# The last step of a gated feed-forward stage: its selection and last product reordered, its result added and stored tile by tile, and a weight split moved one step on

## The chip, the core and the metric

The kernel runs on one core of a Trainium2 chip. The metric is device time in microseconds (us) of one launch, as the median of the runs shown. Engines carry two names: TensorE is PE (its weight loads PEld), VectorE DVE, ScalarE ACT, GpSimd POOL, SyncE SP.

## What is computed

Two transformer-like layers on x of (4, 512, 512), each with an attention part and a feed-forward part behind a layer norm whose scale, shift and gate come from a conditioning vector. The change concerns the feed-forward part of the second layer, cut here to what matters:

```python
def _sparsify_2to4(h):                      # I = 2048
    g = h.reshape(B, S, I // 4, 4)
    a = jnp.abs(g)
    _, idx = jax.lax.top_k(a, 2)
    pos = jnp.arange(4)
    mask = (pos == idx[..., 0:1]) | (pos == idx[..., 1:2])
    return (g * mask.astype(g.dtype)).reshape(B, S, I)
h = silu(x @ w_gate) * (x @ w_up)           # w_gate, w_up: (512, 2048)
y = _sparsify_2to4(h) @ w_down              # w_down: (2048, 512)
...
x = x + gb * y                              # gb: one row of 512 for each batch
```

Of every four neighbouring hidden values the two of larger magnitude are kept, and the output is a float32 array (4, 512, 512).

## The kernel before

One program walks through stages A (attention), B (experts), C (the second layer's first part) and D, the feed-forward part above. `walk` gives each engine the same sequence of steps: in stage D four groups g of 512 hidden columns (the first and the last written out, the middle two a loop), and in each group the four batches b, 512 rows each. Each engine's instructions run in the order in which its own `step_d` emits them; engines meet at semaphores (`wait_ge`, `then_inc`). There is no planner: where an instruction stands in its function is where it stands in its queue.

Every float32 product is made of three matmuls on rounded parts (`mm3`, lines 768 to 772): HI times HI, HI times LO, LO times HI. So each operand is first split: ScalarE copies it rounded (HI), and GpSimd or VectorE subtracts that copy from the value (LO).

A step (g, b) of stage D:

- TensorE computes gate and up for four blocks r (the hidden columns are laid out so that the four members of each group of four sit in blocks 0 to 3), 24 matmuls a block, into banks 0 and 4 or 1 and 5. So block r=2 needs the banks of r=0 back. Then it runs the down product of the step before (`tail_d`, from line 1167): four tiles t of 128 rows, 12 matmuls each, 48 in all, into two banks that take turns (a ring).
- ScalarE applies SiLU to each gate block (L1580), takes absolute values (L1566, into `ab4`), and after the selection makes the HI copies into `ad` (L1605). For the last three groups, step b=0 ends with the HI copies of the down weights (`split_d(g, 4)` and `(g, 5)`, L1235, into W2). Their LO parts are on GpSimd's queue at the end of the same step (L2239). TensorE waits for them at the down product of b=0, which stands in step b=1.
- VectorE multiplies SiLU by up (L2172, into `hh`), then selects: comparisons, maxima and minima of the pairs (0, 1) and (2, 3), flags, and four products of flag and value (L2219). Between these it evacuates the four tiles of the previous down product, times the gate row, into `tmp` (L1898).
- GpSimd adds each `tmp` to x (L2305) and makes the LO parts of `ad` (L2239), but in the last step of all, where VectorE makes them (L2226).
- SyncE loads the raw weights (L560) and stores a finished batch as one transfer of 1024 KB (L754).

The last step (g=3, b=3) has nothing behind it but its own down product: `epi` on TensorE runs it, VectorE evacuates its four tiles, GpSimd adds them, and SyncE stores the batch.

Of the kernel before, what the change touches and what calls it, by code (L numbers as in the profile page):

```python
# [26 lines left out]
ALU = mybir.AluOpType  # L27
# [212 lines left out]
def build(nc, x_in, wa, wbe, wdn, winout, coef, cT, wmod0, wmod1, gwT, bo, norm_w, out, rows_d_):  # L240
# [4 lines left out]
    with ExitStack() as ctx:  # L245
# [124 lines left out]
        hb = [xnb[:, :].rearrange("p (t n) -> p t n", t=NT), h1[:, :, :], h2[:, 0, :, :], h2[:, 1, :, :]]  # L370

# [174 lines left out]
        def _(sp):  # L546
# [204 lines left out]

            def store(b):
# [4 lines left out]
            def epi():  # L757
                store(3)
                sp.wait_ge(out_stored, 16 * NB)
                for stored in row_stored:  # L760
                    sp.wait_ge(stored, 16)
# [5 lines left out]
        def _(pe):  # L767
# [399 lines left out]
            def tail_d(g, b, n0):  # L1167
                s = g * NB + b
                pe.wait_ge(d_lo, s * 4 + 4)
                if b == 0:  # L1170
                    pe.wait_ge(split_done, split_d_at(g, 5) + 1)
                for t in range(NT):
                    o = ring_slot(n0 + t, par_of("D", g, b, t))
                    for r in range(4):
                        last = mm3(o[:, :], lambda h, r=r: ad[:, r, h, t * P:(t + 1) * P],
# [35 lines left out]
        def _(act):  # L1211
# [341 lines left out]
            def step_d(g, b):  # L1553
# [14 lines left out]
                for r in range(4):  # L1568
# [11 lines left out]
                    act.activation(hh[:, r, :], bank[r % 2][:, :], ACT.Silu).then_inc(d_silu, 1)  # L1580
                    if b == 3 and not (isinstance(g, int) and g == GD - 1):
# [16 lines left out]
                if tail_of("D", g, b):  # L1598
                    act.wait_ge(ring_full, ring_before("D", g, b) + NT)
# [3 lines left out]
                for r in range(4):  # L1603
                    act.wait_ge(d_sp, s * NSP + (NSP - 3 + r))
                    act.activation(ad[:, r, HI, :], hh[:, r, :], ACT.Copy).then_inc(d_hi, 1)  # L1605
                if b == 0 and not first:
                    split_d(g, 4)
                    split_d(g, 5)
# [5 lines left out]
        def _(dve):  # L1614
# [548 lines left out]
            def step_d(g, b):  # L2163
# [5 lines left out]
                for r in range(4):  # L2169
                    dve.wait_ge(du_full, s * 4 + (r + 1))  # L2170
                    dve.wait_ge(d_silu, s * 4 + (r + 1))
                    dve.tensor_tensor(hh[:, r, :], hh[:, r, :], bank[4 + r % 2][:, :], ALU.mult).then_inc(d_h, 1)  # L2172
                    if opening and r == 0:
                        add_normed(3, 2)
                        add_normed(3, 3)
                        c_stats(3, 3)
                    if opening and r == 1:
                        c_scales((3, 3))
# [12 lines left out]
                dve.wait_ge(d_abs, s * 4 + 2)  # L2191
                op(tt(c01, a[0], a[1], ALU.is_ge))
                op(tt(mx[:, :], a[0], a[1], ALU.max))
                tail_evac("D", g, b, 0)
                op(tt(a[0], a[0], a[1], ALU.min))
# [4 lines left out]
                tail_evac("D", g, b, 1)  # L2200
                op(tt(a[2], a[2], a[3], ALU.min))
# [393 lines left out]
```

## Time and profile before

| | |
|---|---|
| median of 3 runs | 1926.1 us (1924.27 to 1926.55) |
| profiled execution, as timed | 1928.25 us |
| its span, first to last instruction | 1925.8 us |
| mean granted TensorE clock | 0.970 |
| TensorE busy | 1798.4 us, 93% of the span |
| VectorE busy | 1179.9 us, 61% |
| ScalarE, GpSimd busy | 754.3 and 688.0 us, 39% and 36% |

The rows of a timeline give start, length, engine, line, operation and tiles (output <- inputs, buffer numbers left out), and in brackets how long the engine had been idle and what ended it. Consecutive instructions of an engine may overlap in the record; the distance of two starts is then what an instruction costs. Ends of matmuls are modelled. The granted clock is 1.0 at 2.4 GHz and 0.5 at 1.2 GHz.

### The profile page before, as it was taken

The page shows a single profiled execution, that of the slowest core. Times are in us where ns is not written, and L with a number is a line of the kernel's source. Part 1 is how long each engine was busy: PE and PEld are TensorE (multiplying, and loading weights), DVE is VectorE, ACT ScalarE, POOL GpSimd, SP SyncE. Part 2 cuts the span into 40 slices and gives each one's busy share as a digit, 9 for nine tenths or more (in the row PEclk, how much of TensorE's full clock was granted, in tenths as well). Part 3 has the DMA queues.
Part 4 walks back from the last instruction along what each step waited for, and adds up shares of the span by engine and source line. Part 5 has one row for each costly group of instructions (what it writes and reads, how often), then busy time and mean ns, then how long its engine had stood idle before and what let it go on. Part 6 is the DMA issues. An engine that isn't in the chain of part 4 may idle for free.

```text
span 1925.8 us, 25658 instructions
## 1 busy us (share of the span) xinstructions
PE 1798.4 (93%) x8308; PEld 1406.5 (73%) x8308; DVE 1179.9 (61%) x2152; ACT 754.3 (39%) x1465; POOL 688.0 (36%) x678
## 2 busy tenths in 40 slices
PE   8889999999999999998799999679799999999995
PEld 5556788888888888876566777468688787787784
DVE  5556676666666766677763344556557466575654
ACT  2534455554555555543622222266622213222120
POOL 1335222112222212211253556634536436344442
PEclk9999999999999999999989999889999999999998
DMA  6122353535352544622377998710001101001011
GB/s 246 45 91 82 119 160 92 177 109 197 100 191 81 169 137 142 203 74 75 132 247 216 277 276 222 155 70 26 23 24 50 33 6 55 27 9 51 6 55 44
DMA packets 99905, 216.33 MB, mean 112 GB/s; under 512 B 8456, under 2 KB 33048, under 8 KB 98288
## 3 DMA queue, kind: packets, MB, share of 16 engines
q1 hardware_dynamic: 77696, 166.60, 26.6%
q0 software_dynamic: 11520, 28.96, 6.4%
q10 hardware_dynamic: 10608, 19.74, 3.3%
q8 instruction: 45, 0.74, 0.2%
q14 instruction: 36, 0.29, 0.0%
HBM read 123.93 MB, written 91.35 MB: 112 GB/s over the span
## 4 chain that ended last, share of the span: by engine, by line
PE 68%; DVE 12%; issue 7%; DMA 6%; POOL 3%; ACT 3%; POOLq 0%; ACTq 0%; DVEq 0%; SPq 0%
PE bank L770 19%; PE bank L772 18%; PE bank L771 18%; DMA u_d<-yt,sm 4%; PE bank L1011 2%; PE bank L874 2%; PE bank L1156 2%; DVE hh L2219 2%; PE bank L957 2%; DMA gbt<-mod_rows_d,sm 1%; POOL gbt L2450 1%; DVE rr L1906 1%; PE bank L1018 1%; DVE fl L2197 1%; PE bank L959 1%
## 5 line engine op out<-in xcount | busy, mean ns | idle before, releaser
L1906 DVE RECIPROCAL rr<-rr 128x256 f32<-128x256 f32 x128 | 218.9, 1731 | 0.0
L770 PE MATMUL bank<-hT,W1b 128*128 128x512 f32 x512 | 208.0, 406 | 7.5 <-DVE hh L2172 7.5
L770 PE MATMUL bank<-W1a,hT 128*128 128x512 f32 x512 | 209.8, 410 | 3.4 <-DVE hT L1818 3.4
L771 PE MATMUL bank<-hT,W1b 128*128 128x512 f32 x512 | 203.3, 397 | 0.0
L772 PE MATMUL bank<-hT,W1b 128*128 128x512 f32 x512 | 203.1, 397 | 0.0
L772 PE MATMUL bank<-W1a,hT 128*128 128x512 f32 x512 | 201.5, 394 | 0.0
L771 PE MATMUL bank<-W1a,hT 128*128 128x512 f32 x512 | 200.7, 392 | 0.0
L2305 POOL TENSOR_TENSOR x<-x,tmp 128x512 f32<-128x512 f32 x64 | 101.3, 1583 | 271.5 <-DVE tmp L1898 271.5
L2172 DVE TENSOR_TENSOR hh<-hh,bank 128x512 f32<-128x512 f32 x64 | 43.4, 687 | 196.5 <-PE bank L772 168.5
L1931 DVE SCALAR_TENSOR_TENSOR kt<-bank,kt 128x256 fp32r<-128x256 f32 x128 | 50.8, 397 | 162.4 <-ACT vt L1373 162.2
L2239 POOL TENSOR_TENSOR W<-stage,W 128x1024 fp32r<-128x1024 f32 x32 | 77.1, 2408 | 184.5 <-ACT W L1235 182.2
L1605 ACT ACTIVATE ad<-hh 128x512 fp32r<-128x512 f32 x64 | 40.3, 632 | 254.8 <-DVE hh L2219 254.8
L1372 ACT ACTIVATE kt<-bank 128x256 fp32r<-128x256 f32 x128 | 49.3, 385 | 226.6 <-PE bank L772 226.0
L770 PEld LDWEIGHTS bank<-W1a,hT 128*128 128x128 f32 x512 | 96.7, 189 | 36.5 <-issue 15.5
L770 PEld LDWEIGHTS bank<-hT,W1b 128*128 128x128 f32 x512 | 96.9, 189 | 30.6 <-DVE hh L2172 10.0
L772 PEld LDWEIGHTS bank<-hT,W1b 128*128 128x128 f32 x512 | 96.8, 189 | 23.1
L772 PEld LDWEIGHTS bank<-W1a,hT 128*128 128x128 f32 x512 | 96.8, 189 | 21.8
L771 PEld LDWEIGHTS bank<-hT,W1b 128*128 128x128 f32 x512 | 97.0, 190 | 19.8
L770 PE MATMUL bank<-W1b,ot 128*128 128x512 f32 x256 | 103.4, 404 | 8.2 <-DVE tmp L1895 6.7
L770 PE MATMUL bank<-W,ad 128*128 128x512 f32 x256 | 102.6, 401 | 9.0 <-DVE ad L2226 8.9
L771 PEld LDWEIGHTS bank<-W1a,hT 128*128 128x128 f32 x512 | 97.1, 190 | 17.1
L770 PE MATMUL bank<-hT,W1a 128*128 128x512 f32 x256 | 102.5, 400 | 2.4 <-DVE yn L2133 1.5
(272 smaller groups left out, 4467.4 us busy)
## 6 DMA issues: line engine op xcount, KB each, us to landing
hs_d<-bor SPq DMA_DIRECT2D x24, 1548.0 KB, 11.1
ws_d<-W SPq DMA_DIRECT2D x48, 512.0 KB, 6.1
WB<-ws_d SPq DMA_DIRECT2D x8, 3072.0 KB
stage<-wa SPq DMA_DIRECT2D x32, 512.0 KB
stage<-wbe SPq DMA_DIRECT2D x24, 512.0 KB
stage<-wdn SPq DMA_DIRECT2D x24, 512.0 KB
mw<-wmod SPq DMA_DIRECT2D x10, 1024.0 KB, 4.8
hg<-hs_d ACTq DMA_DIRECT2D x39, 258.0 KB
```

What stands on the lines that cost most here:

```text
L770: pe.matmul(o, lhs(HI), rhs(HI), start=start, stop=False, **kw)
L771: pe.matmul(o, lhs(HI), rhs(LO), start=False, stop=False, **kw)
L772: return pe.matmul(o, lhs(LO), rhs(HI), start=False, stop=stop, **kw)
L874: last = pe.matmul(o[0:NB, :], scT[:, layer, c, :], w[:, c * H:(c + 1) * H], start=c == 0, stop=c == NC - 1)
L957: pe.matmul(o[:, 0:2 * VW], kt[:, t % 2, HI, cols], vt[:, t % 2, :, pair, :], start=t == 0, stop=False, skip_group_check=True)
L1372: act.activation(kt[:, t % 2, HI, :], bank[t % 2][:, 0:256], ACT.Relu)
L1605: act.activation(ad[:, r, HI, :], hh[:, r, :], ACT.Copy).then_inc(d_hi, 1)
L1906: dve.reciprocal(rr[:, pair, h], rr[:, pair, h]).then_inc(r_rec, 1)
L1931: dve.scalar_tensor_tensor(out=kt[:, t % 2, LO, :], in0=bank[t % 2][:, 0:256], scalar=0.0, in1=kt[:, t % 2, HI, :].bitcast(F32), op0=ALU.m ...
L2172: dve.tensor_tensor(hh[:, r, :], hh[:, r, :], bank[4 + r % 2][:, :], ALU.mult).then_inc(d_h, 1)
L2239: return pool.tensor_tensor(dst, src, hi.bitcast(F32), ALU.subtract)
L2305: pool.tensor_tensor(xt, xt, tmp[:, (key + t) % 2, :], ALU.add).then_inc(ring_done, 1)
```

## The change

Two parts. **First**, the two HI splits of the down weights on ScalarE move from the end of step b=0 to step b=1 of the same group, one behind each of the first two SiLUs (groups 1 to 3; group 0 is as it was). GpSimd's part stays where it is in its queue. **Second**, in the last step of all: the selected values are written to `hT` at batch 0's rows, which nobody reads any more, and not to `ad`, so the copies no longer wait for the previous product; VectorE does the first pair's ops before the fourth multiplication; it evacuates the previous product's tiles one place later each, the fourth behind everything; each LO part follows the next selected block; TensorE waits block by block and not for all four; VectorE, not GpSimd, adds the four last tiles to x; and SyncE stores each tile of 256 KB by itself. No matmul is added or taken away, and no bytes.

ScalarE's queue in the last group, from the HI copies of step b=0 into step b=1. Before:

```order
L1605 ACTIVATE ad<-hh 128x512 x4
L1235 ACTIVATE W<-stage 128x1024 x2
L1229 DMA row<-mod_rows_d 128x512
L1580 ACTIVATE hh<-bank 128x512 x2
L1566 ACTIVATE xnb<-hh 128x512
L1580 ACTIVATE hh<-bank 128x512
L1566 ACTIVATE xnb<-hh 128x512
```

Changed:

```order
L1623 ACTIVATE ad<-hh 128x512 x4
L1244 DMA row<-mod_rows_d 128x512
L1595 ACTIVATE hh<-bank 128x512
L1250 ACTIVATE W<-stage 128x1024
L1595 ACTIVATE hh<-bank 128x512
L1250 ACTIVATE W<-stage 128x1024
L1581 ACTIVATE xnb<-hh 128x512
L1595 ACTIVATE hh<-bank 128x512
L1581 ACTIVATE xnb<-hh 128x512
```

`W<-stage` are the two splits: both stood ahead of the first SiLU of b=1 (`hh<-bank`), and now stand behind the first and behind the second.

VectorE's queue in the last step, from the multiplications (`hh<-hh,bank`) on. Before:

```order
L2172 TENSOR_TENSOR hh<-hh,bank 128x512 x4
L2192 TENSOR_TENSOR fl<-xnb 128x512
L2193 TENSOR_TENSOR mx<-xnb 128x512
L1898 TENSOR_TENSOR tmp<-bank,row 128x512
L2195 TENSOR_TENSOR xnb<-xnb 128x512
L2197 TENSOR_TENSOR fl<-xnb 128x512
L2199 TENSOR_TENSOR xnb<-xnb 128x512
L1898 TENSOR_TENSOR tmp<-bank,row 128x512
L2201 TENSOR_TENSOR xnb<-xnb 128x512
L2203 TENSOR_TENSOR fl<-xnb 128x512
```

Changed:

```order
L2209 TENSOR_TENSOR hh<-hh,bank 128x512 x3
L2200 TENSOR_TENSOR fl<-xnb 128x512
L2201 TENSOR_TENSOR mx<-xnb 128x512
L2204 TENSOR_TENSOR xnb<-xnb 128x512
L2209 TENSOR_TENSOR hh<-hh,bank 128x512
L2221 TENSOR_TENSOR fl<-xnb 128x512
L2223 TENSOR_TENSOR xnb<-xnb 128x512
L2226 TENSOR_TENSOR xnb<-xnb 128x512
L1913 TENSOR_TENSOR tmp<-bank,row 128x512
```

The three ops of the first pair (`fl`, `mx`, `xnb`) stand ahead of the fourth multiplication, and the first evacuation (`tmp<-bank,row`) now comes after the second pair's maximum and minimum.

The end of VectorE's queue. Before (an evacuation, four selected blocks, four LO parts, four evacuations):

```order
L1898 TENSOR_TENSOR tmp<-bank,row 128x512
L2219 SCALAR_TENSOR_TENSOR hh<-fl,hh 128x512 x4
L2226 TENSOR_TENSOR ad<-hh,ad 128x512 x4
L1898 TENSOR_TENSOR tmp<-bank,row 128x512 x4
```

Changed:

```order
L1913 TENSOR_TENSOR tmp<-bank,row 128x512
L2252 SCALAR_TENSOR_TENSOR hh<-fl,hh 128x512 x2
L2246 TENSOR_TENSOR hT<-hh,hT 128x512
L2252 SCALAR_TENSOR_TENSOR hh<-fl,hh 128x512
L2246 TENSOR_TENSOR hT<-hh,hT 128x512
L2252 SCALAR_TENSOR_TENSOR hh<-fl,hh 128x512
L2246 TENSOR_TENSOR hT<-hh,hT 128x512 x2
L1913 TENSOR_TENSOR tmp<-bank,row 128x512 x2
L2268 TENSOR_TENSOR x<-x,tmp 128x512
L1913 TENSOR_TENSOR tmp<-bank,row 128x512
```

LO parts (now into `hT`) stand between the selected blocks, the previous product's last evacuation behind the fourth of them, and an addition into x behind each of the last four evacuations (two more pairs follow).

The diff, cut to its core:

```diff
@@ views @@
+        def act_rows(g, b, r, h):
+            if isinstance(g, int) and (g, b) == (GD - 1, NB - 1):
+                return hT[:, h, r, 0:S]
+            return ad[:, r, h, :]
...
@@ SyncE @@
+            def store_tile(t):
+                sp.wait_ge(ring_done, RING[("tail", "D", GD - 1, NB - 1)] + t + 1)
+                n = (NB - 1) * NT + t
+                sp.dma_start(out[NB - 1, t * P:(t + 1) * P, :], x[:, n, :]).then_inc(out_stored, 16)
...
             def epi():
-                store(3)
-                sp.wait_ge(out_stored, 16 * NB)
+                for t in range(NT):
+                    store_tile(t)
+                sp.wait_ge(out_stored, 16 * (NB - 1 + NT))
@@ TensorE, tail_d @@
-                pe.wait_ge(d_lo, s * 4 + 4)
+                ends = isinstance(g, int) and (g, b) == (GD - 1, NB - 1)
+                if not ends:
+                    pe.wait_ge(d_lo, s * 4 + 4)
...
                     for r in range(4):
-                        last = mm3(o[:, :], lambda h, r=r: ad[:, r, h, t * P:(t + 1) * P],
+                        if ends and t == 0:
+                            pe.wait_ge(d_lo, s * 4 + (r + 1))
+                        last = mm3(o[:, :], lambda h, r=r: act_rows(g, b, r, h)[:, t * P:(t + 1) * P],
@@ ScalarE, step_d @@
                     act.activation(hh[:, r, :], bank[r % 2][:, :], ACT.Silu).then_inc(d_silu, 1)
+                    if b == 1 and not first and r < 2:
+                        split_d(g, 4 + r)
...
-                if tail_of("D", g, b):
+                ends = isinstance(g, int) and (g, b) == (GD - 1, NB - 1)
+                if tail_of("D", g, b) and not ends:
                     act.wait_ge(ring_full, ring_before("D", g, b) + NT)
...
-                    act.activation(ad[:, r, HI, :], hh[:, r, :], ACT.Copy).then_inc(d_hi, 1)
-                if b == 0 and not first:
-                    split_d(g, 4)
-                    split_d(g, 5)
+                    act.activation(act_rows(g, b, r, HI), hh[:, r, :], ACT.Copy).then_inc(d_hi, 1)
@@ VectorE, step_d: the first pair's three ops become first_pair() @@
+                def first_pair():
+                    dve.wait_ge(d_abs, s * 4 + 2)
+                    op(tt(c01, a[0], a[1], ALU.is_ge))
+                    op(tt(mx[:, :], a[0], a[1], ALU.max))
+                    if not ends:
+                        tail_evac("D", g, b, 0)
+                    op(tt(a[0], a[0], a[1], ALU.min))
...
                     dve.tensor_tensor(hh[:, r, :], hh[:, r, :], bank[4 + r % 2][:, :], ALU.mult).then_inc(d_h, 1)
+                    if ends and r == 2:
+                        first_pair()
...
+                if not ends:
+                    first_pair()
...
-                tail_evac("D", g, b, 1)
+                if not ends:
+                    tail_evac("D", g, b, 1)
                 op(tt(a[2], a[2], a[3], ALU.min))
+                if ends:
+                    tail_evac("D", g, b, 0)
...
-                tail_evac("D", g, b, 2)
+                tail_evac("D", g, b, 1 if ends else 2)
...
-                tail_evac("D", g, b, 3)
+                tail_evac("D", g, b, 2 if ends else 3)
+
+                def last_lo(r):
+                    dve.wait_ge(d_hi, s * 4 + (r + 1))
+                    dve.tensor_tensor(act_rows(g, b, r, LO), hh[:, r, :], act_rows(g, b, r, HI).bitcast(F32),
+                                      ALU.subtract).then_inc(d_lo, 1)
...
                     op(dve.scalar_tensor_tensor(out=hh[:, r, :], in0=flag, scalar=bound, in1=hh[:, r, :],
                                                 op0=cmp, op1=ALU.mult))
+                    if ends and r >= 1:
+                        last_lo(r - 1)
...
+                if ends:
+                    last_lo(3)
+                    tail_evac("D", g, b, 3)
@@ VectorE, epi @@
                 for t in range(NT):
                     tail_evac("end", GD - 1, 3, t)
+                    n0 = RING[("tail", "D", GD - 1, NB - 1)]
+                    xt = x[:, (NB - 1) * NT + t, :]
+                    dve.wait_ge(ring_read, n0 + t + 1)
+                    dve.wait_ge(ring_done, n0 + t)
+                    dve.tensor_tensor(xt, xt, tmp[:, (n0 + t) % 2, :], ALU.add).then_inc(ring_done, 1)
@@ GpSimd @@
-            def epi():
-                add_tail(("D", GD - 1, 3), RING[("tail", "D", GD - 1, 3)])
-
-            walk(pool, pro, step_a, front, slots, back, step_c, step_d, epi)
+            walk(pool, pro, step_a, front, slots, back, step_c, step_d, lambda: None)
```

## Rows read from the trace of the kernel before

**Rows 1.** The profile page, part 4: shares of the chain that ended last, by engine.

```profile
PE 68%; DVE 12%; issue 7%; DMA 6%; POOL 3%; ACT 3%; POOLq 0%; ACTq 0%; DVEq 0%; SPq 0%
```

**Rows 2.** Who TensorE waited for in the last stage (1380 to 1926): total us, times, longest.

```profile
PE bank L770 <- DVE ad L2226: 8.9, 1, 8.9
PE bank L770 <- DVE hh L2172: 7.5, 7, 1.7
```

**Rows 3.** Timeline, PE, 1798 to 1806: start us, us, what [idle before <-releaser].

```profile
1801.02 0.39 PE L772 MATMUL bank<-hT,W1a 128*128 128x512 f32 x1
1803.11 0.50 PE L770 MATMUL bank<-hT,W1b 128*128 128x512 f32 x1 [1.70 <-DVE hh L2172]
```

**Rows 4.** Timeline, ACT and DVE, from step b=0 to b=1 of the last group.

```profile
1799.25 0.63 ACT L1605 ACTIVATE ad<-hh 128x512 fp32r<-128x512 f32 x1 [1.07 <-DVE hh L2219]
...
1799.79 1.99 ACT L1235 ACTIVATE W<-stage 128x1024 fp32r<-128x1024 f32 x2
1801.68 1.06 ACT L1580 ACTIVATE hh<-bank 128x512 f32<-128x512 f32 x2
...
1802.37 1.28 DVE L2172 TENSOR_TENSOR hh<-hh,bank 128x512 f32<-128x512 f32 x2 [3.15 <-ACT hh L1580]
```

**Rows 5.** Timeline, SP's queue, 1735 to 1800: the last issues of weight loads.

```profile
1736.16 12.58 SPq L560 DMA_DIRECT2D stage<-wdn  x4
```

**Rows 6.** Timeline, DVE, the last step.

```profile
1876.12 0.69 DVE L2172 TENSOR_TENSOR hh<-hh,bank 128x512 f32<-128x512 f32 x1 [5.36 <-PE bank L772]
1881.72 0.69 DVE L2172 TENSOR_TENSOR hh<-hh,bank 128x512 f32<-128x512 f32 x1 [4.91 <-PE bank L772]
...
1884.69 0.69 DVE L1898 TENSOR_TENSOR tmp<-bank,row 128x512 f32<-128x512 f32 x1 [1.08 <-PE bank L772]
...
1885.89 1.78 DVE L2197 TENSOR_TENSOR fl<-xnb 128x512 bf16<-128x512 f32 x1
...
1895.78 3.55 DVE L2219 SCALAR_TENSOR_TENSOR hh<-fl,hh 128x512 f32<-128x512 bf16 x4
1899.25 2.48 DVE L2226 TENSOR_TENSOR ad<-hh,ad 128x512 fp32r<-128x512 f32 x4
```

**Rows 7.** Timeline, ACT and POOL, the last step.

```profile
1882.44 0.63 ACT L1566 ACTIVATE xnb<-hh 128x512 f32<-128x512 f32 x1 [2.40 <-DVE hh L2172]
...
1885.46 1.67 POOL L2305 TENSOR_TENSOR x<-x,tmp 128x512 f32<-128x512 f32 x1 [14.85 <-DVE tmp L1898]
...
1916.24 1.26 POOL L2305 TENSOR_TENSOR x<-x,tmp 128x512 f32<-128x512 f32 x1 [1.51 <-DVE tmp L1898]
```

**Rows 8.** Timeline, PE, first and last of the 48 matmuls of the last product.

```profile
1901.79 0.79 PE L770 MATMUL bank<-W,ad 128*128 128x512 f32 x1 [8.91 <-DVE ad L2226]
...
1915.04 0.40 PE L772 MATMUL bank<-W,ad 128*128 128x512 f32 x1
```

**Rows 9.** Windows: length, busy us (x) of PE, PEld, DVE, ACT, POOL, granted clock, DMA, GB/s.

```profile
1800.00:1808.00 8.00, 6.30 (x28) 4.82 (x27) 1.28 (x2) 4.50 (x7) 6.37 (x4) 1.00 0.10 33
1893.00:1901.70 8.70, 0.00 (x0) 0.00 (x0) 8.70 (x13) 2.46 (x4) 2.61 (x2) 0.69 0.32 121
1901.70:1906.60 4.90, 4.81 (x11) 3.79 (x12) 0.04 (x1) 0.00 (x0) 0.00 (x0) 0.50 0.00 0
```

**Rows 10.** DMA issues over the whole run: times, KB each, median us to landing.

```profile
row<-mod_rows_d ACTq DMA_DIRECT2D x20, 256.0 KB, 3.2
...
out<-x SPq DMA_DIRECT2D x4, 1024.0 KB, 4.3
...
cTs<-cT SPq DMA_DIRECT2D x1, 16.0 KB, 2.1
```

**Rows 11.** Line 245, the block's end: durations in ns, first and last start in us.

```profile
L245 POOLq DRAIN  x1: 9364/9364/9364, 1916.2 to 1916.2; - x1
...
L245 SPq DRAIN  x1: 13/13/13, 1922.0 to 1922.0; - x1
```

More of the change, by code:

```diff
@@ L2168, in step_d @@
                     normed(3, range(NT))
[L2169 to L2178, printed above, removed]
+                ends = isinstance(g, int) and (g, b) == (GD - 1, NB - 1)
                 done = [0]
@@ L2190, in step_d @@
                 tt = dve.tensor_tensor
[L2191 to L2195, printed above, removed]
+                def first_pair():
[5 more added lines that the diff above has]
+                    op(tt(a[0], a[0], a[1], ALU.min))
+                for r in range(4):
+                    dve.wait_ge(du_full, s * 4 + (r + 1))
+                    dve.wait_ge(d_silu, s * 4 + (r + 1))
+                    dve.tensor_tensor(hh[:, r, :], hh[:, r, :], bank[4 + r % 2][:, :], ALU.mult).then_inc(d_h, 1)
+                    if ends and r == 2:
+                        first_pair()
+                    if opening and r == 0:
+                        add_normed(3, 2)
+                        add_normed(3, 3)
+                        c_stats(3, 3)
+                    if opening and r == 1:
+                        c_scales((3, 3))
+                if not ends:
+                    first_pair()
                 dve.wait_ge(d_abs, s * 4 + 4)
@@ L2220, in step_d @@
                                                 op0=cmp, op1=ALU.mult))
+                    if ends and r >= 1:
+                        last_lo(r - 1)
                 assert done[0] == NSP
-                if isinstance(g, int) and g == GD - 1 and b == NB - 1:
-                    for r in range(4):
-                        dve.wait_ge(d_hi, s * 4 + (r + 1))
-                        dve.tensor_tensor(ad[:, r, LO, :], hh[:, r, :], ad[:, r, HI, :].bitcast(F32),
-                                          ALU.subtract).then_inc(d_lo, 1)
+                if ends:
+                    last_lo(3)
+                    tail_evac("D", g, b, 3)
             def epi():
@@ L2533, in step_d @@
                     pool.wait_ge(d_hi, s * 4 + (r + 1))
-                    lo_part(ad[:, r, LO, :], hh[:, r, :], ad[:, r, HI, :]).then_inc(d_lo, 1)
+                    lo_part(act_rows(g, b, r, LO), hh[:, r, :], act_rows(g, b, r, HI)).then_inc(d_lo, 1)
                 if b == 0 and not first:
```

## The prediction

> **What bounds the kernel now.** I read the shares of the chain that ended last first: TensorE carries 68% of it and VectorE 12% [rows 1]. So only two kinds of edit can pay: those that close gaps on TensorE, and those that shorten what stands behind its last product. The list of TensorE's waits then shows the gaps in the last stage [rows 2]: one of 8.9 us, released by VectorE's remainders (ad), and seven short ones of 7.5 us together, released by VectorE's gate times up (hh). The short ones lie at the third of the four blocks r, where bank 0 must be free. Three of the seven belong to step b=1 of groups 1 to 3, of one size; the one of group 3, 1.70 us, stands for the three [rows 3]. The last step I then followed in the timeline, engine by engine, and the end of the program in the queue entries of the block's end; their rows come with their terms.
>
> **The down split moved from b=0 to b=1.** At the end of step b=0 ScalarE copies the last selected block at 1799.25, and 0.54 us later starts two split copies of W2, 1.99 us; only then comes the first SiLU of b=1 (1801.68), VectorE's multiplication (1802.37) and TensorE's third block (1803.11) [rows 4, 3]. With the splits behind, the SiLU starts at 1799.79, the multiplication 0.69 later at 1800.48, and TensorE may go 0.74 later at 1801.22. Its previous matmul began at 1801.02 and at full clock 28 matmuls fill 6.3 us [rows 9], 0.23 us from one to the next, so it would go on at 1801.25: the gap closes with nothing left over. I count 1.8 us for each of the three, idle time and the restart together: **5.4 us** (4.9 if only the idle time goes). Each step's selection starts from TensorE's own last block, so a step that begins earlier also ends earlier; the other four short gaps stay.
>
> What the moved copies now hold up: each stands ahead of the next SiLU. The second SiLU comes 1.0 us later than it could, about 1801.3, its multiplication at 1802.0; TensorE wants that bank with the fourth block, 5.6 us after the third (24 matmuls), at 1806.9. That leaves 4.1 us. GpSimd's two W2 remainders follow ScalarE's copies at about the same time as now, since four remainders of ad stand before them on its queue; TensorE wants W2 with the down product some 13 us later. The loads are not moved: SyncE issued the last weight loads of group 3 by 1748.7, and ScalarE splits W2 from 1799.79 on [rows 5, 4]. Cost zero.
>
> **The last step.** Two comparisons and the minimum of the first pair go ahead of the fourth multiplication, where VectorE now idles 4.91 us (1876.8 to 1881.72) [rows 6]. Three ops of 0.6 us fit there: free. The next comparison (c23) waits for ScalarE's last absolute, 1882.44 plus 0.63 [rows 7], so it starts at 1883.1 and not at 1885.89. From there I lay the ops out as they are spaced now. An op has 0.6 us (0.34 in bf16). After each evacuation GpSimd adds for 1.67 us, and the VectorE op that meets it is stretched, c23 from 0.69 to 1.78 us [rows 6, 7]: 1.1 us per meeting, four of them now. Before the first selected block stand three evacuations where four stood; two meetings lie there and a third just behind. That gives: c23 1883.1, first evacuation 1885.1, second 1888.0, third 1891.3, first selected block 1892.0 to 1892.7, second one stretched to 1894.3, first remainder done at 1894.9. TensorE's last product no longer waits for all four remainders but for the first: it starts at **1895.0** and not at 1901.79 [rows 8], 6.8 us sooner. The other remainders come at 1896.1, 1897.3 and 1898.15 (each waits for ScalarE's copy, 0.63), which gates rows r=1, 2, 3 of the first tile; from then 39 matmuls at 0.23 us are left. The values written to rows of hT of their own mean that ScalarE no longer waits until the previous product (it ends at about 1892.9) has read ad; this only just mattered in the new order.
>
> **The clock.** Now the product runs from 1901.79 to 1915.44, 13.65 us for 48 matmuls, because TensorE idled 8.9 us before it: the granted clock fell in the gap to the lower level (0.69 as a mean over it), and the first eleven matmuls ran at 0.50, 1.2 GHz [rows 8, 9]. In the new order the gap is 2.1 us, then comes work with breaks of 0.5 us. The 1.70 us gap left the clock at 1.00 [rows 9]. I take full clock: the product ends at 1898.2 plus 39 times 0.23 and the last one's flow, 1907.5. Gain at the product's end **7.9 us**; at half clock from the first matmul it would take its 13.65 us again and end at 1908.6, gain 6.8.
>
> **The last sum and the store.** After TensorE's end come 0.7 us of evacuation and GpSimd's addition of 1.26 us, until 1917.50 [rows 8, 7]. The addition moves to VectorE: the nearest rows are its float32 remainders with two SBUF operands, four in 2.48 us [rows 6], so 0.69 with the wait's gap: **0.5 us** gained. VectorE has 2.8 us per tile for 1.5 us of work. The store: 1024 KB land 4.3 us after issue. Now each tile has its own, and only the last, 256 KB, is at the end; it has no row. The nearest are a 256 KB load with 3.2 and a 16 KB load with 2.1 [rows 10]. The output store is fast for its size, four times the bytes of the row load in 1.1 us more, so I take 2.2: **2.1 us** gained, 1.1 to 2.2. The three other stores have 2.8 us each and their issue costs SyncE about 0.4; their cover is TensorE's product. A rule speaks against this edit: the Trainium skill ("DMA: Bandwidth & Descriptors", sections "Anatomy of one DMA" and "Rules for kernel authors") gives every transfer about 2.0 us plus bytes over 436 GB/s and advises to coalesce small ones. By it the last store takes 2.6 us, an estimate, against 4.4 for the whole, and the sum would gain 1.8 here.
>
> **The exit.** This is the part that the chain of waits hides. The final store has landed by about 1921.8 and SyncE has drained at 1922.0 [rows 11], but the span ends at 1925.8. What holds it is GpSimd's closing DRAIN, 9.36 us from 1916.2 to 1925.6 [rows 11]; its last addition ended at 1917.50 [rows 7], so it runs 8.1 us beyond it. In the changed kernel GpSimd's last instruction is the addition for the step before, which ends about 1900.5, so its drain would be over at 1908.6, before the last store lands at 1911.2. The 4.1 us between landing and end shrink to about 0.4: **3.7 us**. This holds only if the drain is counted from GpSimd's own last work. If something after the store's landing sets it, nothing comes here.
>
> **Sum.** 5.4 + 7.9 + 0.5 + 2.1 + 3.7 = 19.6 us. Against the profiled execution's own span of 1925.8 us this gives 1906.2 (1928.25 as timed gives 1908.6); against the median of the runs, 1926.1, it gives **1906.5 us**. The profiled run was 2.15 us above that median, and the three runs spread over 2.3 us; about 0.2%, 3.9 us, is what a measurement of this kernel can tell from no change.
>
> **Rivals.**
> *The exit stays.* GpSimd's drain ends late whatever it did before. Against it: the drain began right behind the last addition. For it: no second instance in the trace tells its length. 3.7 us less gain: 1910.2.
> *The clock falls.* The gap and the broken run behind it may be too little work. For it: in the 8.9 us gap it did fall. It costs 1.1 us, if the first tile's rows are gated anyway, and 2.3 us, the excess of the present product over 48 matmuls at 0.23, at worst: 1907.6 to 1908.8.
> *The gaps come back elsewhere.* VectorE's chain of a step takes about as long as TensorE's cover; if that binds in b=1 the three gaps stay: 1911.9. Against it: steps b=2 have no wait of TensorE in that list, and their ScalarE order is the new one without the splits.
> *Slower.* A W2 load that is late now holds ScalarE ahead of the second SiLU, thus the fourth block, in three steps. Beyond the 4.1 us of slack each microsecond costs three. To eat 19.6 us and 3.9 more, a load must come 12 us after ScalarE asks for it: 1930.0. Against it: the loads are issued some 50 us ahead, and ScalarE's first split in b=0 follows its copy at once, without a wait for one.
>
> **How the numbers follow.** Forecast 0.55, the clock falls 0.18, the exit stays 0.17, the gaps come back 0.05, slower 0.03, and 0.02 that several of these together leave nothing to be seen. The forecast's own range is 1905.0 to 1908.0, from the bounds of the store (1.1), of the gaps (0.5) and of the meetings with GpSimd (one more or less, 1.1). With the clock and the exit the range is 1904.8 to 1911.0. Faster by over 0.2% 0.95, within 0.2% 0.02, slower 0.03.
>
> **What would show it.** TensorE's waits in the last stage: four on hh, some 2.5 us together, not seven; the one before the last product 2 us long; granted clock 1.00 in it; VectorE's c23 about 1.4 us behind the fourth multiplication (4.2 now); last store landing near 2.2 us; span ending under 1 us after it, with a GpSimd drain that began some 12 us before the end. A gap above 3 us before the last product, a drain that still ends the span, or waits at b=1 would prove the corresponding step wrong.

## The result and the profile after

The changed kernel took 1904.8 us (median of four runs, 1899.5 to 1907.9), the kernel before, beside it, 1925.2 (four runs, 1920.9 to 1926.6): a ratio of 0.9887 with a 95% interval of 0.9865 to 0.9909. Applied to the 1926.1 us of before, that is 1904.3 us: 2.2 below the forecast and 0.5 below the low end of the range. (The ratio of the two medians alone is 0.9894, which would be 1905.7 us and inside the range.) A second comparison at the end of the study, six runs of the changed kernel against eleven of before, gave 0.9898 [0.9874, 0.9922], the ratio of the forecast (1906.5 over 1926.1). The profiled execution of the first took 1907.86 us with a span of 1905.8; forecast was a span of 1906.2.

The chain of the page, part 4, against [rows 1]: TensorE's share rose from 68 to 76%, VectorE's fell from 12 to 9%.

```profile
PE 76%; DVE 9%; issue 4%; DMA 4%; POOL 3%; ACT 2%; ACTq 0%; POOLq 0%; DVEq 0%; SPq 0%
```

TensorE's waits in the last stage (1380 to 1926), against [rows 2]: in us, times, longest. Seven waits on hh have become four, and 8.9 us before the last product 2.2, now on the values in rows of hT. The first line, 7.0 us once near the stage's start, where the transposes of a layer norm wait for ScalarE, is not among [rows 2] and not among the gaps that the prediction lists, although the kernel before has it too (at 1383.1); no edit touches it.

```profile
PE bank L826 <- ACT tmp L1296: 7.0, 1, 7.0
PE bank L781 <- DVE hh L2209: 2.5, 4, 1.0
PE bank L781 <- DVE hT L2246: 2.2, 1, 2.2
```

From step b=0 to b=1 of the last group, timeline of ScalarE and VectorE (start, us, engine, line), against [rows 4]. The SiLU L1595 follows the copy L1623 after 0.54 us and each split copy L1250 stands behind a SiLU. VectorE's multiplication comes 1.23 us behind the start of that copy; in [rows 4] it came 3.12 behind. TensorE's block then follows without a gap.

```profile
1795.14 0.63 ACT L1623 ACTIVATE ad<-hh 128x512 fp32r<-128x512 f32 x1 [1.07 <-DVE hh L2252]
...
1795.68 0.58 ACT L1595 ACTIVATE hh<-bank 128x512 f32<-128x512 f32 x1
1796.16 1.05 ACT L1250 ACTIVATE W<-stage 128x1024 fp32r<-128x1024 f32 x1
1797.11 0.58 ACT L1595 ACTIVATE hh<-bank 128x512 f32<-128x512 f32 x1
```

```profile
1796.37 0.69 DVE L2209 TENSOR_TENSOR hh<-hh,bank 128x512 f32<-128x512 f32 x1 [1.26 <-ACT hh L1595]
```

VectorE in the last step, timeline, against [rows 6]. The first pair's three operations (L2200 to L2204) lie in what was idle time, c23 (L2221) comes 1.39 us behind the fourth multiplication and no longer 4.17, and the comparison with mx (L2232) is the one that GpSimd's first addition stretches.

```profile
1870.71 0.68 DVE L2200 TENSOR_TENSOR fl<-xnb 128x512 bf16<-128x512 f32 x1
...
1875.71 0.69 DVE L2209 TENSOR_TENSOR hh<-hh,bank 128x512 f32<-128x512 f32 x1 [3.11 <-PE bank L783]
1877.10 0.69 DVE L2221 TENSOR_TENSOR fl<-xnb 128x512 bf16<-128x512 f32 x1 [0.70 <-ACT xnb L1581]
...
1880.23 1.78 DVE L2232 TENSOR_TENSOR fl<-mx,xnb 128x512 bf16<-128x512 f32 x1
...
1885.32 0.68 DVE L1913 TENSOR_TENSOR tmp<-bank,row 128x512 f32<-128x512 f32 x1
1885.92 2.36 DVE L2252 SCALAR_TENSOR_TENSOR hh<-fl,hh 128x512 f32<-128x512 bf16 x2
```

GpSimd in the same stretch: four additions for the step before, the last of them now the last thing it does.

```profile
1879.80 1.67 POOL L2342 TENSOR_TENSOR x<-x,tmp 128x512 f32<-128x512 f32 x1 [15.18 <-DVE tmp L1913]
...
1892.75 1.28 POOL L2342 TENSOR_TENSOR x<-x,tmp 128x512 f32<-128x512 f32 x1 [5.03 <-DVE tmp L1913]
```

The last product's first and last matmul, timeline of TensorE, against [rows 8], and under it the windows, against [rows 9] (length, busy us of PE, PEld, DVE, ACT, POOL, granted clock, DMA share, GB/s). The clock was 1.00 in the 2.16 us gap, and fell right behind it, to 0.57 as a mean over 3.9 us.

```profile
1889.02 0.47 PE L781 MATMUL bank<-W,hT 128*128 128x512 f32 x1 [2.16 <-DVE hT L2246]
...
1901.54 0.39 PE L783 MATMUL bank<-W,hT 128*128 128x512 f32 x1
```

```profile
1886.90:1889.00 2.10, 0.00 (x0) 0.01 (x1) 2.10 (x3) 0.99 (x2) 0.82 (x1) 1.00 0.00 0
1889.00:1892.90 3.90, 3.88 (x10) 2.58 (x11) 3.58 (x6) 1.26 (x2) 0.15 (x1) 0.57 0.00 0
1892.90:1896.00 3.10, 3.10 (x15) 2.58 (x14) 1.39 (x2) 0.00 (x0) 1.14 (x1) 0.99 0.34 128
```

The last addition (VectorE's timeline), the landing of the four tile stores (line 760, min/median/max) and the queue entries of the block's end against [rows 11]. GpSimd's closing DRAIN is as long as before, but it begins at 1892.7 and is over some 3.7 us before the span ends.

```profile
1902.68 0.69 DVE L2268 TENSOR_TENSOR x<-x,tmp 128x512 f32<-128x512 f32 x1
```

```profile
DMA to landing us min/median/max: 2.0/2.0/3.5
```

```profile
L245 POOLq DRAIN  x1: 9384/9384/9384, 1892.7 to 1892.7; - x1
...
L245 SPq DRAIN  x1: 13/13/13, 1905.6 to 1905.6; - x1
```

### The profile page after: what moved, and what is told of

The parts are those of the page before. It is cut to its first block, busy times and chain, and to the rows that moved or that the text cites. A ratio compares the mean times of both kernels' runs of the same rounds, so it can differ in the third digit from the quotient of the medians.

```text
span 1905.8 us, 25664 instructions
## 1 busy us (share of the span) xinstructions
PE 1799.1 (94%) x8308; PEld 1406.2 (74%) x8308; DVE 1182.5 (62%) x2156; ACT 753.2 (40%) x1465; POOL 681.9 (36%) x674
## 4 chain that ended last, share of the span: by engine, by line
PE 76%; DVE 9%; issue 4%; DMA 4%; POOL 3%; ACT 2%; ACTq 0%; POOLq 0%; DVEq 0%; SPq 0%
PE bank L781 22%; PE bank L783 21%; PE bank L782 21%; PE bank L1022 3%; PE bank L1167 2%; PE bank L885 2%; DMA u_d<-yt,sm 2%; PE bank L968 2%; DVE hh L2252 1%; POOL hs_d L2426 1%; DVE rr L1921 1%; PE bank L970 1%; ACT tmp L1296 1%; PE bank L826 1%; POOL gbt L2487 1%
## 5 line engine op out<-in xcount | busy, mean ns | idle before, releaser
L2342 POOL TENSOR_TENSOR x<-x,tmp 128x512 f32<-128x512 f32 x60 | 95.8, 1596 | 254.2 <-DVE tmp L1913 254.2
L1623 ACT ACTIVATE ad<-hh 128x512 fp32r<-128x512 f32 x60 | 37.8, 632 | 240.3 <-DVE hh L2252 240.3
L781 PE MATMUL bank<-W1b,ot 128*128 128x512 f32 x256 | 103.4, 404 | 8.3 <-DVE tmp L1910 6.8
L783 PE MATMUL bank<-W1b,ot 128*128 128x512 f32 x256 | 101.3, 396 | 0.0
```

The source lines that it names most:

```text
L781: pe.matmul(o, lhs(HI), rhs(HI), start=start, stop=False, **kw)
L783: return pe.matmul(o, lhs(LO), rhs(HI), start=False, stop=stop, **kw)
L2342: pool.tensor_tensor(xt, xt, tmp[:, (key + t) % 2, :], ALU.add).then_inc(ring_done, 1)
```

## The experiments

Executions of one program differed by several us, more than most terms of the sum: in the last comparison, eleven of before took from 1920.3 to 1932.3 us and six of the changed kernel from 1900.3 to 1912.4. So besides the times, each trace was divided at the same five places, from the start and end times of its timeline rows. one_store, late_pool, warm, warm_more, dve_adds and abs_first were each run once, so that their times alone say little and the stretches carry the argument:

```
us                 first mult.  to last   to first    length of  to end   to end
                   starts at    mult.     matmul of   last       of last  of span
                                          last prod.  product    add.
before             1351.8       529.90    20.07       13.65      2.06     8.30
split_only         1355.2       524.55    20.08       13.26      2.06     8.27
tail_only          1349.8       530.16    13.32       13.40      1.46     2.42
after              1351.0       524.68    13.31       12.91      1.44     2.43
after_again        1351.6       524.79    13.30       13.05      1.45     2.42
one_store          1348.7       525.96    13.32       12.75      1.45     4.70
late_pool          1350.5       524.52    13.32       12.87      1.45     8.46
warm               1345.8       524.79    13.25       12.33      1.45     2.41
warm_more          1351.0       524.73    13.23       12.67      1.45     2.40
dve_adds           1354.1       524.80    11.43       12.68      1.46     2.46
abs_first          1356.0       524.90    13.31       13.01      1.45     2.43
best               1346.6       520.48    11.42       12.26      1.45     2.42
```

"First mult." is VectorE's first gate times up of the last stage, "last mult." the one of the last step's fourth block. All names but before are the labels of the runs below.

### The two parts apart

The first kernel has the move of the split alone, the second the changed last step alone.

```diff
 # split_only: before, with
+                    if b == 1 and not first and r < 2:
+                        split_d(g, 4 + r)
...
-                if b == 0 and not first:
-                    split_d(g, 4)
-                    split_d(g, 5)
 # tail_only: the changed kernel, with this taken back
```

> The kernel before with the two W2 copies moved alone. My theory (each gap at b=1 closes whole, nothing comes back): the three TensorE gaps of 1.6 to 1.7 us are gone from the list of waits, four of 2.5 us together stay, and from VectorE's first multiplication of the stage to its last one there are 5.4 us less (5.3 in the changed kernel against the one before). Time 5.4 us less, ratio 0.9972. Rival (the gaps come back behind): six or seven gaps stay and the ratio is 1.000.

> The changed kernel with the W2 copies put back to the end of b=0. Theory: the rest of the gain, about 14.5 us of the sum (13.3 us from the last multiplication to the last product instead of 20.1; product, addition, store and exit as in the changed kernel), ratio 0.9925. The two parts lie in different steps, so this one and the other one alone add up to the whole. Rival (the measured gain of over 20 us has a part that my terms do not name, brought by one of the two edits): one of the two comes out over 2 us better than said, in its trace too. Second rival (it is the spread between executions before the last stage): both traces show the terms and the medians miss them by 1 to 3 us either way.

Measured: split_only 1921.2 us, ratio 0.9967 [0.9957, 0.9978], 6.4 us less on 1926.1 (from 4.2 to 8.3); tail_only 1914.3 us, ratio 0.9934 [0.9919, 0.9950], 12.7 us less (9.6 to 15.6). Together they make 19.1 us; the whole change brought 21.8 in the first comparison and 19.6 in the second. In the traces the split took 5.35 us off the stretch between the multiplications and no more than 0.4 off any stretch behind it, and the last step's edits took 13.5 us off what follows the fourth multiplication (44.08 to 30.60). TensorE's waits, first of split_only, then of tail_only, show each part to do its own work and no more:

```profile
PE bank L770 <- DVE ad L2225: 8.9, 1, 8.9
...
PE bank L770 <- DVE hh L2171: 2.6, 4, 1.0
```

```profile
PE bank L781 <- DVE hh L2210: 7.5, 7, 1.7
...
PE bank L781 <- DVE hT L2247: 2.3, 2, 2.2
```

### The store and the exit

one_store joins the last four tile stores again. late_pool leaves all else alone, but makes GpSimd wait for the last addition and write one element, so that its last instruction comes late.

```diff
 # one_store
-                for t in range(NT):
-                    store_tile(t)
-                sp.wait_ge(out_stored, 16 * (NB - 1 + NT))
+                store(3)
+                sp.wait_ge(out_stored, 16 * NB)
 # late_pool
+            def epi():
+                pool.wait_ge(ring_done, RING[("tail", "D", GD - 1, NB - 1)] + NT)
+                pool.memset(mark[:, 0:1], 0.0)
```

> The changed kernel, but with one transfer of 1024 KB for the last batch at the end. Theory: from its issue to the landing 4.2 us instead of 2.0, and the end of the span 2.2 us later, measured from the last addition. Rival (end set by GpSimd's drain, as in the kernel before): the drain ends about 1902.1 on the changed kernel's clock, before this store lands, so the rival gives 0.

> The changed kernel with one memset of 4 bytes on GpSimd behind the last addition; nothing reads it. Theory (GpSimd's closing drain lasts some 8.1 us beyond its own last instruction, whatever that is): the span ends about 8.2 us after the last addition, not 2.4: 5.8 us slower. Rival (the drain was long because of the addition or of the store's landing): under 1 us slower.

Measured: one_store 1908.9 us, late_pool 1913.2, one run each. From the last addition to the end of the span it took 2.43 us in the changed kernel, 4.70 with one store (2.27 more) and 8.46 with the late GpSimd (6.03 more). Of one_store, the landing of its four 1024 KB stores (min/median/max); the edge moved by just the difference to the 2.0 of a tile:

```profile
DMA to landing us min/median/max: 4.2/4.3/4.8
```

Of late_pool, GpSimd's timeline at the end and the queue entries. The store has landed and SyncE has drained by 1904.9; GpSimd's DRAIN, begun with a 0.09 us write, lasts 8.15 us and the span ends with it.

```profile
1902.70 0.09 POOL L2578 MEMSET mark<- 1x1 f32 x1 [9.37 <-DVE x L2268]
```

```profile
L245 POOLq DRAIN  x1: 8154/8154/8154, 1902.7 to 1902.7; - x1
L245 SPq COMPARE_BRANCH  x1: 41/41/41, 1904.7 to 1904.7; - x1
L245 SPq DRAIN  x1: 13/13/13, 1904.9 to 1904.9; - x1
```

So the drain ends some 8.1 us behind GpSimd's last operation, be it an addition of 1.26 or 1.28 us or a write of 0.09. In before and in late_pool it set the end; there a faster store would have brought nothing. The 5.87 us that the change took off this place come from two edits: moving the last additions off GpSimd, without which the drain sets the end and the tile stores are worth nothing, and the tile stores, without which 2.3 us are given back.

### The clock

warm fills the gap before the last product with eight matmuls of full size into a bank that is written over afterwards; warm_more adds two more ahead of each of the three later waits of the first tile.

```diff
                         if ends and t == 0:
+                            for _ in range(8 if r == 0 else 0):
+                                pe.matmul(bank[6][:, :], wdd[:, HI, 0, 0:P], wdd[:, HI, 0, :], start=True, stop=True)
                             pe.wait_ge(d_lo, s * 4 + (r + 1))
 # warm_more: 8 if r == 0 else 2
```

> The changed kernel with 8 matmuls of W2 by itself into bank 6, which nobody reads, in the 2.2 us gap before the last product. Theory (the clock fell in the changed kernel because TensorE idled 2.2 us and then worked with breaks): the granted clock stays 1.00 through the product, which then ends 11.8 to 12.4 us after its first own matmul, and not 12.9. Rival (it falls by the breaks alone, or by where the moment lies): 12.7 to 13.4 again. From the last multiplication to the span's end 29.2 against 30.1 us.

> As warm, with 2 further unread matmuls ahead of each of the three following waits of the first tile. Theory: clock 1.00 throughout; each pair takes 0.45 us of a break of some 0.5 us, so the product ends as in warm or up to 0.3 us later. Rival (only the breaks matter): warm still falls and this one does not.

Measured: warm 1902.1 us, warm_more 1907.7 (one run each; 5.3 of the 5.6 us between them lie in front of the last stage, see the first column). The gap was 0.24 us instead of 2.16, the start of the product as before (13.25 behind the fourth multiplication), and the granted clock stayed full. Windows of warm over the fillers and the first half of the product:

```profile
1884.00:1886.00 2.00, 1.73 (x6) 0.78 (x5) 2.00 (x4) 1.04 (x2) 0.00 (x0) 1.00 0.00 0
1886.00:1889.00 3.00, 2.79 (x12) 2.14 (x13) 2.14 (x4) 0.22 (x1) 1.29 (x1) 1.00 0.00 0
1889.00:1893.00 4.00, 4.00 (x19) 3.33 (x18) 2.08 (x3) 0.00 (x0) 0.00 (x0) 1.00 0.80 301
```

The product took 12.33 us, 0.6 to 0.7 less than in the two traces of the changed kernel, and from the last multiplication to the span's end it took 29.4 us (29.2 expected). The fillers in the short breaks of warm_more brought nothing on top: its product took 12.67, 0.3 longer than warm's.

The other traces bear the theory out. Six have the gap of 2.15 us and the breaks behind it, and in all six the granted clock fell to the lower level in the product. Four have a gap of 0.24 to 0.27 us (warm, warm_more, and dve_adds and best below, which close it without fillers) and, but for warm_more, unfilled breaks behind it; in all four the clock stayed at 1.00. So the breaks alone don't bring it down. What the fall costs depends on where it lies. The first tile's rows wait for VectorE's remainders at either clock, so slow matmuls are nearly free there and cost time only behind it:

```
us            clock falls, after the    length of
              product's first matmul    product
one_store     0.15                      12.75
late_pool     0.38                      12.87
after         0.52                      12.91
abs_first     0.69                      13.01
after_again   0.79                      13.05
tail_only     1.67                      13.40
```

Against 12.33 us at full clock that is 0.4 to 1.1 us.

### GpSimd's additions in VectorE's chain

In dve_adds VectorE itself adds the four tiles of the step before, in the last step only, so that GpSimd touches nothing while it selects.

```diff
+                def add_prev(t):
+                    if not ends:
+                        return
...
+                    dve.tensor_tensor(xt, xt, tmp[:, n % 2, :], ALU.add).then_inc(ring_done, 1)
...
                 op(tt(fa, mx[:, :], a[2], ALU.is_ge))
+                add_prev(0)
...
                 op(tt(fs, fa, fb, ALU.add))
+                add_prev(1)
...
-                tails("D", g, b)
+                if not (isinstance(g, int) and (g, b) == (GD - 1, NB - 1)):
+                    tails("D", g, b)
```

> The changed kernel with the four additions of step (3, 2)'s result on VectorE and not on GpSimd. Theory (each GpSimd addition stretches the VectorE op that it meets by 1.1 us, three of them ahead of the first remainder): three stretches go, two additions of 0.6 us come ahead of the first remainder: from the last multiplication to the product's start 11.2 to 11.8 us, not 13.3. Rival (the stretch is not GpSimd's doing but the op's own): 14.5 us, the additions on top.

Measured: 1909.0 us in one run (with a late first multiplication, 1354.1); from the last multiplication to the span's end 28.0 us, and not 30.1. The last product started 11.43 us behind the fourth multiplication, 1.88 sooner, although VectorE had two more operations of 0.6 us in the chain. Timeline of VectorE: the comparison with mx (L2232 in the changed kernel, there 1.78 us) has 0.68 again.

```profile
1882.80 0.68 DVE L2239 TENSOR_TENSOR fl<-xnb 128x512 bf16<-128x512 f32 x1
1883.40 0.68 DVE L2241 TENSOR_TENSOR fl<-mx,xnb 128x512 bf16<-128x512 f32 x1
1884.00 0.68 DVE L2205 TENSOR_TENSOR x<-x,tmp 128x512 f32<-128x512 f32 x1
```

So the three meetings ahead of the first remainder had cost 3.1 us (1.88 plus twice 0.6), close to three times the 1.1 us that the prediction had read from [rows 6]. The product took 12.68 us here, though the clock stayed full: the third addition stands ahead of the last remainder, which the first tile waits for.

### The four gaps that stayed

The changed kernel still has four waits on hh, 2.5 us together: three at a step b=0 that follows a step b=3 (0.7 to 1.0 us), one of 0.16 in the last step. My theory was that ScalarE's copies of the next group's weights hold up the absolute values there. abs_first moves each copy behind the absolute.

```diff
-                    if b == 3 and not (isinstance(g, int) and g == GD - 1):
-                        act.wait_ge(du_full, s * 4 + (r + 1))
-                        split_d(g + 1, r)
...
-                absolute(3)
+                    if r == 3:
+                        absolute(3)
+                    if b == 3 and not (isinstance(g, int) and g == GD - 1):
+                        act.wait_ge(du_full, s * 4 + (r + 1))
+                        split_d(g + 1, r)
```

> The changed kernel with ScalarE's weight copies in step b=3 behind the absolute values and not ahead of them. Theory (the gaps of 0.7 to 1.0 us at the third block of b=0 in groups 1 to 3 come from the late last absolute, 0.75 us): those three gaps go, one of 0.2 us stays, and from first to last multiplication of the stage there are 522.0 us instead of 524.6. Rival (they come from the loop's register work or from late loads): no change.

Measured: 1913.0 us in one run; the stretch between the multiplications was 524.90 us, as without the edit, and all four waits were there. The theory fell. TensorE's waits in abs_first:

```profile
PE bank L781 <- DVE hh L2210: 2.6, 4, 1.0
```

Its timeline shows what stands there instead: in step b=3 of the second group GpSimd works from 1613.49 to 1617.60 without a break (the W1b remainder, then an addition), and VectorE's minimum and comparison are stretched to 1.93 and 1.77 us, while the evacuation at 1613.91, which reads a bank, keeps its 0.69. VectorE first, then GpSimd:

```profile
1613.91 0.69 DVE L1914 TENSOR_TENSOR tmp<-bank,row 128x512 f32<-128x512 f32 x1 [0.91 <-PE bank L783]
1614.52 1.93 DVE L2205 TENSOR_TENSOR xnb<-xnb 128x512 f32<-128x512 f32 x1
1616.37 1.77 DVE L2222 TENSOR_TENSOR fl<-xnb 128x512 bf16<-128x512 f32 x1
```

```profile
1613.49 2.40 POOL L2277 TENSOR_TENSOR W1b<-stage,W1b 128x1024 fp32r<-128x1024 f32 x1 [3.95 <-ACT W1b L1250]
1615.84 1.76 POOL L2343 TENSOR_TENSOR x<-x,tmp 128x512 f32<-128x512 f32 x1
```

### The additions moved in every step b=3

best gives VectorE the additions of the step before in all steps b=3, not the last alone. Against dve_adds one more thing differs: in the last step the third addition, like the fourth, stands behind the last remainder. It was measured on the same chip as the changed kernel again (five runs of best, six of after_again).

```diff
 # best against dve_adds
                 def add_prev(t):
-                    if not ends:
+                    if b != NB - 1:
                         return
...
+                if not ends:
+                    add_prev(2)
                 tail_evac("D", g, b, 2 if ends else 3)
+                if not ends:
+                    add_prev(3)
...
-                    if ends and r == 3:
-                        add_prev(2)
...
                     tail_evac("D", g, b, 3)
+                if ends:
+                    add_prev(2)
                     add_prev(3)
...
-                if not (isinstance(g, int) and (g, b) == (GD - 1, NB - 1)):
+                if b != NB - 1:
                     tails("D", g, b)
```

> The changed kernel with the previous product's additions on VectorE in every step b=3 (in the last one the third and fourth behind the last remainder). Theory (what stretches VectorE is GpSimd's additions): in the last step the product starts 11.4 us after the last multiplication and not 13.3, and is done 0.5 us quicker; in steps (0..2, 3) four meetings of 1.1 us give way to four additions of 0.6, so the gaps of 0.7 to 1.0 us at b=0 shrink or go, 522.5 to 523.5 us from first to last multiplication and not 524.7. About 4 us faster than the changed kernel, ratio to the kernel before 0.9875. Rival (the steps' gaps have another cause): 524.7 us, and only the last step's 2.4 us are gained.

> The changed kernel itself again, more often and on the chip of the run beside it. Theory (my terms are right in size, 20.0 us in the traces, and the first comparison's 1.13% was the spread of what comes before the last stage): ratio 0.9896, that is 1906.1 us beside 1926.1; the first multiplication of the last stage lies anywhere from 1346 to 1356 us. Rival (the edits bring 1 to 2 us that no term names): ratio 0.9887 again or less.

Measured: best 1899.7 us (1896.5 to 1902.4), ratio to before 0.9870 [0.9849, 0.9890]; after_again 1907.0 us (1900.3 to 1912.4), ratio 0.9898 [0.9874, 0.9922]. The medians are 7.2 us apart. The two intervals overlap slightly, so the times alone don't settle it, but the traces do: 4.3 us between the multiplications (524.79 to 520.48) and 2.7 behind them (30.22 to 27.55) make 7.0. The direction was as expected, but the size wasn't: 522.5 to 523.5 us were expected between the multiplications, and some 4 us in all. The waits of TensorE on hh are gone, 2.5 of those 4.3 us; the rest I didn't resolve. From 1380 us on this is all that best waits for (its layer norm's 7.0 us lie just ahead, at 1377.8):

```profile
PE bank L781 <- DVE hT L2262: 0.7, 3, 0.3
```

The W1b remainder still stretches one operation of VectorE in each of the first three steps b=3 (below that of the second group, timeline of best). So the gaps go with GpSimd's additions alone, though its remainders are still there.

```profile
1601.63 2.89 DVE L2211 TENSOR_TENSOR mx<-xnb 128x512 f32<-128x512 f32 x1
```

## Why the prediction was wrong, and where it was right

What failed is the step **How the numbers follow**: it worked the range out from the bounds of the terms alone and put the spread between executions of one program at nothing. The mechanism, the effects of the edits and the sum itself held up, apart from the clock. The sum's terms, forecast and measured, the latter from the table of stretches, before against after:

| step | forecast | measured |
|---|---|---|
| gaps at b=1 | 5.4 | 5.2 (split_only 5.35) |
| last product starts sooner | 6.8 | 6.76 |
| last product is shorter, the clock being full | 1.1 | 0.74 |
| last addition on VectorE | 0.5 | 0.62 |
| store | 2.1 | 2.2 |
| exit | 3.7 | 3.7 |
| ahead of the last stage | 0 | 0.8 |
| sum | 19.6 | 20.0 |

- **The total** is 20.0 partly by luck. The last 0.8 us lie where no edit reaches, and without them the terms make 19.2.
- **The gaps** closed as worked out, without a rest, and no W2 load was late. The rivals of gaps that come back and of a late load are out.
- **The last step** followed the laid-out order to within 0.2 us: from c23 to the first evacuation 1.9 (2.0 forecast), to the third 8.2 (8.2), to the first selected block 8.8 (8.9), and 11.9 to the first matmul, as forecast. The price of a meeting with GpSimd carried this, and dve_adds bore it out.
- **The clock** is the one term whose mechanism failed: "I take full clock". It held through the 2.16 us gap, as [rows 9] suggested from the 1.70 us one, and fell right behind it. So the rival "the clock falls" was what happened, at 0.6 to 0.7 us (12.91 and 13.05 against 12.33 with the clock full) in the two traces of the changed kernel and not at its 1.1 us, which only tail_only paid. The excess against the forecast's 12.5 was 0.4 us. This made the kernel slower than forecast, so it can't be why the time fell below the range. The rival's worst case, 2.3 us, doesn't come out of its own working either: 13.65 us less 48 matmuls at 0.23 is 2.6.
- **The store** landed in 2.0 us, not 2.2, from 4.3. With the fit in the Trainium skill ("DMA: Bandwidth & Descriptors", "Anatomy of one DMA") it would have been 2.6, an estimate from the page; here the measurement is lower and decides. The prediction takes that fit for every transfer, but the section's heading gives it for transfers that GpSimd issues, and these stores are SyncE's. The advice on the same page ("Rules for kernel authors") to coalesce many small transfers doesn't carry over to this place, where only the last piece is on the path: one_store gave back 2.3 us.
- **The exit** came as reasoned from one instance, and late_pool brought the second: the drain follows GpSimd's own last operation.

Back to the step that failed. The range was built from the bounds of my terms alone, and its low end of 1904.8 left 1.7 us below the forecast. It isn't even their sum: the store (0.1 faster or 1.0 slower), the gaps (0.5 slower) and the meetings (1.1 either way) make 1905.3 to 1909.1, where the text has 1905.0 to 1908.0. Above all, the text itself noted runs that spread over 2.3 us and a measurement that can tell 3.9 us from nothing, and put neither into the range. The second comparison fell on the forecast's ratio and the first 0.0011 below it, with the forecast inside its interval: both are the same kernel, and their intervals, each over 0.4% wide, are wider than the whole range (0.9889 to 0.9922 as ratios). That the second fell exactly on the forecast is luck too: its interval spans gains from 15.0 to 24.3 us. Half the first interval is 0.0022, or 4.2 us; a range that begins that far under the forecast, at 1902.3, would have held both. The three faster runs of the first comparison left no trace, so that their times are lower by this spread and not by a term is inferred from the two traces of the changed kernel, which show the terms alike, and isn't shown directly.

Where that spread arises the first column of the table of stretches shows. Nothing that any of the edits touches runs before the last stage, and still its first multiplication starts between 1345.8 us (warm) and 1356.0 (abs_first). Some 4 us of it are there when the stage of the slots (part of the experts, stage B) begins, and 7 more arise in it: VectorE's 39 operations on yt span 193.0 us in warm and 199.8 in abs_first (and 198.8 in before). Rows of the yt operations, warm, then abs_first, with first and last start:

```profile
L2063 DVE SCALAR_TENSOR_TENSOR yt<-bank,sm,gbt x39: 750/751/754, 1035.0 to 1228.0; 128x512 f32<-128x512 f32 x39
```

```profile
L2062 DVE SCALAR_TENSOR_TENSOR yt<-bank,sm,gbt x39: 749/751/753, 1038.9 to 1238.7; 128x512 f32<-128x512 f32 x39
```

What differs inside that stage stays open: no experiment was made on it. Nothing points at the change: before (1351.8) and split_only (1355.2) lie within the ten other traces, and the changed kernel's own two (1351.0 and 1351.6) lie beside that of before.

## What to carry to other kernels

Look at what ends the span behind the last store: an engine whose closing drain is long, as GpSimd's 8.1 us here, must do its last work early, and only then does a finer last store pay. A short operation that stands alone between two engines' chains can cost more by stretching its neighbour than by its own length, so ask who runs beside it before giving work to the idle engine; here giving 16 additions to VectorE, the busier of the two, won 7 us in the traces. And a range must hold the spread between executions of the same program, beside the bounds of the terms.

## What the runs showed of the hardware

- GpSimd's closing DRAIN ends about 8.1 us behind its last operation: 9.36 us from 1916.2 behind an addition of 1.26 [rows 7, 11], 9.38 behind one of 1.28, 8.15 behind a write of 0.09. ScalarE's and VectorE's take 0.66 and 0.73.
- A GpSimd addition of 128x512 (f32) and a VectorE operation beside it with both inputs in SBUF stretch each other: 0.68 to 1.78 us on VectorE, 1.28 to 1.67 on GpSimd. An operation that reads a bank kept its 0.69 beside GpSimd: the evacuation at 1613.91 in abs_first, and in the changed kernel, from 1400 us on, all 23 multiplications by a bank (gate times up) that had over 0.2 us beside an operation of GpSimd's.
- The granted clock held 1.00 in a gap of 2.16 us and fell to the lower level behind it, while TensorE worked with breaks (six traces). With the gap at 0.24 to 0.27 us it stayed up in spite of the breaks (four traces). Eight filler matmuls in the gap made the product 0.6 us shorter, and the product started no later for them (13.25 us behind the last multiplication, 13.31 without).
- A store of 256 KB issued by SyncE landed 2.0 us after its issue (three of four; 3.5 for the first, behind a 1024 KB one), one of 1024 KB 4.2 to 4.8.
